# Three instructions moved ahead in two queues, and score matmuls set apart, in a two-layer graph kernel

## The reference

```
def layer(h, params):                      # h: [128, 128, 384]
    u = einsum('bid,bjd->bij', h, h) / sqrt(384)
    a = softmax(u, axis=-1)
    delta = a * adjacency_matrix
    attn = delta / (sum(delta, axis=-1) + 1e-10)
    hl, hs, hr = h @ wl.T + b_l, h @ ws.T + b_s, h @ wr.T + b_r
    ctx = (attn * upper) @ hl + diag(attn) * hs + (attn * lower) @ hr
    o = (ctx - mean) / sqrt(var + 1e-12) * g + beta
    return relu(o)
out = layernorm(x + layer2(layer1(x)))     # eps 1e-5
```

## Time and profile before

| | us |
|---|---|
| median of 3 runs | 1613.95 (1612.61 to 1614.08) |
| the profiled execution, its own time | 1614.73 |
| its span | 1613.0 |
| TensorE matmuls busy | 1594.6 (99%) |
| TensorE weight loads busy | 1571.5 (97%) |
| VectorE busy | 1396.4 (87%) |
| GpSimd busy | 1294.1 (80%) |
| ScalarE busy | 1079.3 (67%) |

### The profile page before, as it was taken

One profiled execution on the slowest core, in us unless ns is written; L12 is line 12 of the kernel. 1 busy time (PEld: TensorE's weight loads), 2 busy tenths in 40 slices (PEclk: granted clock), 3 DMA queues, 4 the chain that ended last, 5 costly groups with the idle time before them and its releaser, 6 DMA issues.

```text
span 1613.0 us, 35972 instructions
## 1 busy us (share of the span) xinstructions
PE 1594.6 (99%) x9267; PEld 1571.5 (97%) x9267; DVE 1396.4 (87%) x4490; ACT 1079.3 (67%) x2958; POOL 1294.1 (80%) x1665
## 2 busy tenths in 40 slices
PE   9999999999999999999999999999999999999996
PEld 8999999999999999999999999999999999999995
DVE  7788888888888888888888888888888888888887
ACT  6566666666666666666666666666666666666665
POOL 6788888888888888888888888888888888888874
PEclk9999999999999999999999999999999999999998
DMA  5555555555555555555555555555555555555541
GB/s 180 125 132 138 129 133 135 132 133 130 134 132 135 129 137 131 133 130 139 127 133 130 138 129 133 133 134 133 130 134 131 135 129 139 130 133 129 135 108 49
DMA packets 589175, 211.28 MB, mean 131 GB/s; under 512 B 473952, under 2 KB 572256, under 8 KB 589152
## 3 DMA queue, kind: packets, MB, share of 16 engines
q1 hardware_dynamic: 490752, 198.91, 47.8%
q10 hardware_dynamic: 98400, 12.11, 4.9%
HBM read 128.98 MB, written 81.92 MB: 131 GB/s over the span
## 4 chain that ended last, share of the span: by engine, by line
PE 97%; DVE 1%; POOL 1%; ACT 1%; issue 0%; DMA 0%; SPq 0%; DVEq 0%; POOLq 0%; ACTq 0%
PE p_proj L464 74%; PE p_gather L591 17%; PE p_score L458 5%; DMA w_raw<-WT 0%; POOL proj_split L299 0%; POOL w L1351 0%; DVE proj L767 0%; DVE p_gather L725 0%; DVE p_gather L733 0%; DVE stats L702 0%; DVE p_gather L698 0%; ACT proj_split L1062 0%; PE p_score L482 0%; DVE y L739 0%; POOL rstd L1304 0%
## 5 line engine op out<-in xcount | busy, mean ns | idle before, releaser
L464 PE MATMUL p_proj<-w,hT_layer 128*128 128x384 f32 x6912 | 1345.7, 338 | 0.0
L464 PEld LDWEIGHTS p_proj<-w,hT_layer 128*128 128x128 f32 x6912 | 1193.7, 188 | 0.5 <-POOL w L1351 0.3
L299 POOL TENSOR_TENSOR proj_split<-proj,proj_split 128x768 fp32r<-128x768 f32 x253 | 467.1, 1846 | 88.4 <-ACT proj_split L1062 88.4
L591 PE MATMUL p_gather<-proj_split,attnT_split 128*128 128x384 f32 x1536 | 322.5, 344 | 2.2 <-issue 2.2
L767 DVE TENSOR_TENSOR proj<-p_proj,bias_all 128x768 f32<-128x768 f32 x256 | 243.9, 953 | 71.6 <-PE p_proj L464 71.6
L1300 POOL TENSOR_TENSOR attnT_split<-attnT,attnT_split 128x256 fp32r<-128x256 f32 x256 | 190.2, 743 | 142.8 <-ACT attnT_split L1053 142.7
L591 PEld LDWEIGHTS p_gather<-proj_split,attnT_split 128*128 128x128 f32 x1536 | 263.0, 188 | 21.8 <-POOL attnT_split L1300 14.3
L1304 POOL TENSOR_TENSOR rstd<-veps,neg_half 128x1 f32<-128x1 f32 x384 | 208.7, 549 | 52.7 <-DVE veps L711 39.6
L1062 ACT ACTIVATE proj_split<-proj 128x768 fp32r<-128x768 f32 x256 | 213.0, 832 | 5.8 <-DVE proj L767 4.8
L458 PE MATMUL p_score<-hT_layer 128*128 128x256 f32 x768 | 215.6, 281 | 1.1 <-DVE hT_layer L754 0.8
L1066 ACT ACTIVATE normed<-gathered,nbias,rstd 128x384 f32<-128x384 f32 x128 | 90.7, 709 | 141.5 <-POOL nbias L1308 141.5
(11 more groups left out here) (69 smaller groups left out, 1677.7 us busy)
## 6 DMA issues: line engine op xcount, KB each, us to landing
swap_mem<-blocks SPq DMA_DIRECT2D x124, 256.0 KB, 2.2
whole<-swap_mem SPq DMA_DIRECT2D x496, 64.0 KB, 2.5
xt_raw<-xT SPq DMA_DIRECT2D x128, 192.0 KB, 2.6
xn<-x SPq DMA_DIRECT2D x128, 192.0 KB, 2.6
out<-o SPq DMA_DIRECT2D x128, 192.0 KB, 2.0
rows_mem<-rows_blocks SPq DMA_DIRECT2D x123, 192.0 KB, 1.9
adj_layer<-adj SPq DMA_DIRECT2D x256, 64.0 KB, 2.1
rowsT<-rows_mem SPq DMA_DIRECT2D x246, 48.0 KB, 2.5
```

What stands on the lines that cost most here:

```text
L299: op.tensor_tensor(proj_split[u][:, LO], proj[u][:, UP:LOW + 1, :], proj_split[u][:, HI].bitcast(F32), ALU.subtract).then_inc(s_proj_lo[k], 1)
L464: return nc.tensor.matmul(p_proj[:, which, 0:D], hT_of(k, b)[:, slot, st, c, :], w[:, k, which, mv, c, :], start=(n == 0), stop=(n == 8))
L591: last = nc.tensor.matmul(home(k, b)[:, 0:D], AT_split[u][:, st, side, :], proj_split[u][:, mv, side, :], start=(side == UP and n == 0), s ...
```

## The change

It is an edit of order; every computation stays.

- ScalarE: `copy_cross(i)` and `high_sides(1, i - 4)` run before the exponentials, in this order, and no longer behind them in the other order. `copy_cross` gets a wait for `s_cross_sum`, GpSimd's addition that reads the `crossed` of the iteration before. At the end of an iteration `high_projections(1, i - 3)` runs before `finish`.
- VectorE: `turn_cross` runs before the masks. Since a mask's transposition is now the last that fills `blocks`, SyncE's store waits for `s_attn_blocks[1]`, and `s_cross_blocks` goes.
- TensorE: the three `score_late` matmuls stand behind side projection 16 and self projections 0 and 2, in place of self projections 0, 1 and 2.

```diff
                     sp.wait_ge(s_attn_blocks[0], 1)
-                elif last == 4:
-                    sp.wait_ge(s_cross_blocks, i - 3)
                 else:
                     sp.wait_ge(s_attn_blocks[1], i - 2)
...
+                    if late is not None and n == 16:
+                        score_late(*late, 0)
...
-                    if late is not None:
-                        score_late(*late, n)
+                    if late is not None and n in (0, 2):
+                        score_late(*late, 1 + n // 2)
...
-                    project_sides(0, i, r, 1, i - 4, range(18), early=rest)
+                    project_sides(0, i, r, 1, i - 4, range(18), early=rest, late=(i - 2, p))
                     project_self(0, i, r, 1, i - 4, late=(i - 2, p))
...
+                turn_cross(i, p)
                 if live(i, i + 1):
                     mask(i, 0, i + 1, q)
                 mask(i, 1, i - 3, q)
-                turn_cross(i, p)
                 diagonal(1, i - 3, q)
...
             def copy_cross(i):
+                if not isinstance(i, int) or i > 4:
+                    done(act, s_cross_sum, i - 5)
...
                 normalise_rows(i, i - 1)
+                copy_cross(i)
+                high_sides(1, i - 4)
                 exponentials(1, i - 3, q)
                 if live(i, i + 1):
                     exponentials(0, i + 1, q)
-                high_sides(1, i - 4)
-                copy_cross(i)
                 high_projections(0, i)
...
                     output_squares(i - 5, q)
+                high_projections(1, i - 3)
+                if live(i, i - 5):
                     finish(i, q)
-                high_projections(1, i - 3)
```

More of the change, by code:

```diff
@@ L203, in graph_block @@
         s_crossed = sem("s_crossed")
-        s_cross_blocks = sem("s_cross_blocks")
         s_cross_sum = sem("s_cross_sum")
@@ L504, in score_late @@
                         done(pe, s_kept, b1 - 3)
[L505 to L508, removed]
+                step = score_step(1, b1, slot1, n)
+                if n == C - 1:
+                    step.then_inc(s_parts[1], 1)
             def project_sides(k, b, slot, before, b_last, steps, scored=None, first=0, last_part=14,
-                              early=None):
+                              early=None, late=None):
                 if 0 in steps:
@@ L790, in turn_cross @@
                     nc.vector.transpose(blocks[:, slot, 2:4].rearrange("p k n -> p (k n)"),
-                                        crossed[:].rearrange("p k n -> p (k n)")).then_inc(s_cross_blocks, 1)
+                                        crossed[:].rearrange("p k n -> p (k n)"))
                 else:
-                    nc.vector.transpose(blocks[:, slot, 3], crossed[:, 1]).then_inc(s_cross_blocks, 1)
+                    nc.vector.transpose(blocks[:, slot, 3], crossed[:, 1])
             def mask(i, k, b, slot):
```

## The result

The change makes the kernel 1.0% faster: 1597.27 us (1596.02 to 1597.66, 5 runs) against 1613.95, ratio 0.9897, 95% interval 0.9882 to 0.9911. The forecast was 1602.0 with a range from 1600 to 1608; the direction was right, but 16.7 us were won where 12 were forecast. The time lies outside the range.

A forecast was written before the change was run, and what follows sets the result against it. TensorE's matmuls, 99% of the span, were taken as the bound, with gather(1)'s late weight load to win: 1614.73 - 12.2 + 0.3 = 1602.8 us, as a median 1602.0; 80% range 1600 to 1608.

The forecast's parts named there:

- The gather's wait: At gather(1), the first weight load waits 0.16 us for GpSimd's subtraction; curing it wins 122 x 0.10 = 12.2 us.
- room: In the new order GpSimd's subtraction ends 0.49 us before TensorE can begin gather(1)'s load.
- the 92 waits of the list: Listed waits of `p_gather` loads for `attnT_split`, 14.3 us in 92 cases; the forecast counted 122 iterations instead.
- the spacing: Layer 2's scores two projections apart: last score's time unchanged, taken as zero, bounds 0 and 0.12 us loss per iteration.
- The first pass: At i = 4 the exponentials wait some 0.9 us for the cross copy; costs 0 to 0.9 us once, taken as 0.3.
- The edits costed at nothing: ScalarE's projection copy ahead of `finish` fills idle time; VectorE's crossed transposition hides in its wait for exponentials; both cost zero.
- Rival 3: Masks pushed 0.30 us, nothing absorbs it before `p_gather`; layer 2's first score load is late: 1627 us, chance 0.08.
- Rival 1's signal: Side-projections-done signal 0.12 us later carries round VectorE's queue, delaying `hT_layer` at the first score: 1607 us, chance 0.15.
- the 0.06 us that are free: On TensorE, about 0.06 us of a weight load's lateness costs the matmul stream nothing.

The follow-up runs named there:

- order alone: Changed kernel with layer 2's score matmuls put back behind self projections 0, 1 and 2, new ScalarE and VectorE order kept: 1600.29 us, ratio 0.9922.
- second profile: The unaltered changed kernel timed and profiled once more on another occasion: 1597.60 us, ratio 0.9901, period 12.221 us.
- spacing alone: Kernel before, with only layer 2's scores moved behind side projection 16 and self projections 0 and 2: 1633.21 us, ratio 1.0129.
- projection copy first: Kernel before, with only `high_projections(1, i - 3)` moved ahead of `finish` on ScalarE: 1612.73 us, ratio 1.0000.
- finish first: Changed kernel with `finish` ahead of `high_projections(1)` again, as in the kernel before: 1626.62 us, ratio 1.0079.
- adjacent: Changed kernel with layer 2's three score matmuls directly behind each other, after self projection 2: 1599.10 us, ratio 0.9908.
- order with finish first: Changed kernel with scores back behind self projections 0, 1 and 2, and `finish` ahead of `high_projections(1)` again: 1600.49 us, ratio 0.9921.
- close one later: Changed kernel with scores one projection apart, behind self projections 1, 2 and 3: 1599.65 us, ratio 0.9914.
- one later: Changed kernel with each late score one projection later, behind side projection 17 and self projections 1 and 3: 1594.38 us, ratio 0.9885.

## Why the prediction was wrong

**The gather's wait: right.** Load late by 0.16, cause, cure and room (0.54 against 0.49) are as read. The load was late in every one of the 121 iterations, 170 ns behind the start of the matmul before it on average, so taking all of them and not the 92 waits of the list was right. The term was 122 x 0.10 = 12.2; the order alone measured 12.4, and the distances of the gather fell by 111 ns, 13.5 us in 122 iterations. The rule of the Trainium skill, "TensorE: Matmul & The Clock Gate", section "The mechanism", by which a load overlaps no matmul of the same rows, would have given no gain here. The measurement decides against it: loads start 2 to 5 ns after the start of the matmul before them, and the gain came. The same section of the Trainium skill also lets a load for the background weight buffer go ahead of matmuls in flight, and that sentence would not have spoken against the change; no run here shows which buffer these loads use.

**The term that failed is the spacing.** The step reads "the columns and the time of the last score are unchanged", and was costed at zero, with bounds of 0 and a loss of 0.12. A gain was excluded without a row for it. The row was there: fifteen projections 0.176 apart behind the scores I took for the normal pace. Against the order alone, the spacing gains 12.238 - 12.210 = 0.028 us per iteration, 122 x 0.028 = 3.4 us (3.4 and 4 by the ratios of the two timings, 2.1 by the second profile). With 3.4 the sum would have been 1598.6, and a range lower by as much, 1596.6 to 1604.6, would have held the time. The other 1.3 us are the gather's, 13.5 against 12.2.

**The first pass.** 0.3 us were taken, from 0 to 0.9. In the profile of the changed kernel the pass from gather(1) of i = 4 to that of i = 5 took 64.62 - 50.50 = 14.12 us, against 63.95 - 50.68 = 13.27 before. But this belongs to the execution and not to the change: in its second profile the same kernel took 13.32, and the spacing alone, without the later copies, took 13.99. The wait at gather(0, 4), first in the one profile, then in the other:

```profile
56.43 1.28 PE L589 MATMUL p_gather<-proj_split,attnT_split 128*128 128x384 f32 x6 [1.55 <-issue]
```

```profile
55.80 1.28 PE L589 MATMUL p_gather<-proj_split,attnT_split 128*128 128x384 f32 x6 [0.78 <-issue]
```

ScalarE's issue of row loads started at 51.33 in the first, 2.5 us after SyncE's store of `rows_blocks` was issued (48.81), and at 50.83 in the second, 1.9 us after it (48.94). The cross copy did wait 0.88 us there, near the 0.9 of the prediction, but 0.78 against the 0.74 before is all that reached TensorE. A cost of the first pass is not shown.

**The edits costed at nothing.** As single edits they are: the projection copy first gives 1.0000. But taken out of the changed kernel it costs 29 us, and the transposition costs 29 too. I wrote both off as hidden, which was right for the sum and wrong for the reason: they keep loops short that the new order and the new score places would otherwise have made the bound. Rival 3 (1627, the masks pushed by 0.30 with nothing to absorb it) is what happens without the transposition's move, at 1626 and 1627. Rival 1's signal, 0.12 later, is by my reading behind most of the 20 us lost with the spacing alone, and it is what puts the first score into the loop of "finish first". In the whole change it is hidden, as forecast, but only just: the first score's load comes 46 ns behind the start of the matmul before it on average, inside the 0.06 us that are free.

**What stays open.** Why projections behind close scores start unevenly is not shown. The loads are not visibly behind: in the means of starts they begin 2 to 5 ns after the matmul before them in both cases. The traces do show that a stretch is either even or uneven as a whole. Taking the mean of the distances behind the last score in each of 120 iterations, close scores whose first load is in time give 176.7 to 176.9 ns in 119 or 120 of them (the kernel before, order alone, projection copy first, adjacent, order with finish first, close one later). In the changed kernel 26 iterations are like that (34 in its second profile) and the others lie between 173.4 and 174.1; with the scores one later it is 1. In those 26 the first score's load comes 47 to 67 ns behind the start of the matmul before it, and in that one 67, where 5 is the mean. So two apart, unevenness goes with a first load that is slightly late, though not every late load brings it; this is a part of the 24 ns per iteration between the changed kernel and "one later". How a late load does it stays open, too.

## What to carry to other kernels

When an engine is 99% busy, compare the start-to-start distance of its like instructions in several places; the least one found is the normal pace, and every stretch above it is a term, also where the reordering seems neutral. In a software pipeline with five queues, a part tried alone says little: of the three tried alone here, one gave nothing and two cost 19 and 20 us, and the whole wins 17. A wait that appears inside a loop over engines costs not its lateness once but the loop's length less the period, at each iteration; so for each moved instruction follow its value round to the next iteration, and ask also which signal now stands behind it in its queue: moving one score from behind side projection 17 to before it was enough to close such a loop here. Before calling a term of a few tenths of a microsecond that occurs once the work of a change, look at a second profile of the same kernel.

## What the runs showed of the hardware

Over the iterations, a weight load that starts 0.17 us behind the start of the matmul before it costs TensorE's stream 0.10 us; one 0.32 behind costs 0.25. So some 0.07 us of lateness are free; in the changed kernel a score's load that is 0.05 behind on average costs the two distances about it 4 ns. Matmuls of 384 columns start 0.173 us apart at best, and 0.179 and 0.174 in turn behind score matmuls of 256 columns that stand adjacent or with one projection between, up to the next gather. Behind scores two apart the same stretch is even in 119 of 120 iterations when the first score's load is in time, and uneven in 26 and 34 of 120 when it is some 0.05 us late. ScalarE's issue of row loads starts 1.90 us after the end of the transposition whose rows SyncE stores for it, in all seventeen profiles.
